# The slots' bias taken into phi before the logits, in place of two bias products per bank

## What is computed

```python
x = x + xattn(layernorm(x), ctx, Wq, Wk, Wv, Wo)         # softmax over 1500 keys, 16 heads
h = layernorm(x)                                          # no affine part: every row sums to 0
logits = (einsum('tzd,ed->tze', h, phi_w) + phi_b).reshape(t, z, 64, 32)
D = softmax(logits, axis=3);  C = softmax(logits, axis=2)
X = einsum('tznp,tzd->npd', D, h)                         # then clip, layernorm, tanh
Y = einsum('npd,ndH->npH', tanh(...), expert_w) + expert_b
x = x + einsum('tznp,npH->tzH', C, Y)
```

## Time and profile before

| | |
|---|---|
| median of 3 runs | 433.64 us |
| the profiled execution: its own time | 433.6 us |
| its span, first to last instruction | 431.7 us |
| PE (TensorE) busy | 422.8 us, 98% |
| DVE (VectorE) busy | 333.9 us, 77% |
| ACT (ScalarE) busy | 245.2 us, 57% |
| POOL (GpSimd) busy | 167.7 us, 39% |
| granted TensorE clock | 1.00 |

### The profile page before, as it was taken

One profiled execution on the slowest core, in us unless ns is written; L12 is line 12 of the kernel. 1 busy time (PEld: TensorE's weight loads), 2 busy tenths in 40 slices (PEclk: granted clock), 3 DMA queues, 4 the chain that ended last, 5 costly groups with the idle time before them and its releaser, 6 DMA issues.

```text
span 431.7 us, 7476 instructions
## 1 busy us (share of the span) xinstructions
PE 422.8 (98%) x3004; PEld 388.5 (90%) x3004; DVE 333.9 (77%) x612; ACT 245.2 (57%) x412; POOL 167.7 (39%) x98
## 2 busy tenths in 40 slices
PE   7999999999999999999999999999999999999897
PEld 5898999999999999889999998899999898999887
DVE  3788756875786778767898689978988899669981
ACT  2576647665664546654673766466655564644641
POOL 6409800524050405032608053617146443456710
DMA  7401110213020011110120012101000010296000
GB/s 203 143 16 14 33 58 14 57 44 100 14 53 33 20 14 22 64 18 14 14 73 20 12 14 72 20 12 15 2 18 14 0 14 18 53 260 176 2 2 23
DMA packets 15418, 19.05 MB, mean 44 GB/s; under 512 B 4032, under 2 KB 10960, under 8 KB 15384
## 3 DMA queue, kind: packets, MB, share of 16 engines
q1 hardware_dynamic: 15384, 18.58, 17.3%
HBM read 18.32 MB, written 0.26 MB: 43 GB/s over the span
## 4 chain that ended last, share of the span: by engine, by line
PE 82%; DVE 11%; ACT 5%; DMA 1%; issue 0%; SPq 0%; ACTq 0%
PE turned L736 16%; PE acc L756 8%; PE acc L757 8%; PE acc L758 8%; PE scores L720 8%; PE scores L726 8%; PE scores L723 8%; PE misc L773 3%; PE misc L642 2%; DVE pT_l L1424 2%; ACT prob L1170 2%; DVE small L1414 2%; PE scores L1100 2%; PE misc L800 2%; ACT logit L1221 1%; ACT pT_h L1163 1%
## 5 line engine op out<-in xcount | busy, mean ns | idle before, releaser
L1163 ACT CAST pT_h<-turned 125x512 fp32r<-125x512 f32 x168 | 95.3, 591 | 124.1 <-PE turned L736 123.5
L1424 DVE TENSOR_TENSOR pT_l<-turned,pT_h 125x512 fp32r<-125x512 f32 x168 | 112.3, 686 | 60.2 <-ACT pT_h L1163 59.5
L1414 DVE TENSOR_REDUCE small<-scores 128x1 f32<-128x500 f32 x168 | 108.1, 674 | 4.4 <-PE scores L726 4.1
L736 PE MATMUL turned<-ident,prob 128*125 128x128 f32 x672 | 94.6, 276 | 1.9 <-DVE pT_l L1424 1.6
L736 PEld LDWEIGHTS turned<-ident,prob 128*125 128x125 f32 x672 | 87.5, 187 | 9.5 <-DVE pT_l L1424 3.5
L756 PE MATMUL acc<-pT_h,ctx_nh 125*128 125x256 f32 (+1 forms) x288 | 94.1, 327 | 0.0
L1170 ACT ACTIVATE prob<-scores,small 128x1500 f32<-128x1500 f32 x56 | 85.0, 1518 | 10.2 <-DVE small L1417 9.8
L758 PE MATMUL acc<-pT_h,ctx_nl 125*128 125x256 f32 (+1 forms) x288 | 86.5, 300 | 0.0
L757 PE MATMUL acc<-pT_l,ctx_nh 125*128 125x256 f32 (+1 forms) x288 | 86.3, 300 | 0.0
L720 PE MATMUL scores<-ctx_th,qk_h 128*128 128x500 f32 x168 | 67.7, 403 | 0.4 <-ACT prob L1170 0.4
L726 PE MATMUL scores<-ctx_th,qk_l 128*128 128x500 f32 x168 | 65.3, 389 | 0.0
(11 more groups left out here) (216 smaller groups left out, 567.8 us busy)
## 6 DMA issues: line engine op xcount, KB each, us to landing
ctx_raw<-in_ctx_dram SPq DMA_DIRECT2D x7, 750.0 KB
rbc<-rden_row SPq DMA_DIRECT2D x15, 128.0 KB, 3.3
rbc<-rden_row SPq DMA_DIRECT2D x8, 192.0 KB, 3.2
eb<-in_L_ffn_expert_b_dram SPq DMA_DIRECT2D x4, 256.0 KB, 5.6
ctx_raw<-in_ctx_dram SPq DMA_DIRECT2D x3, 224.0 KB, 4.9
wq_sb<-in_L_xattn_Wq_dram SPq DMA_DIRECT2D x2, 256.0 KB, 4.6
wk_sb<-in_L_xattn_Wk_dram SPq DMA_DIRECT2D x2, 256.0 KB, 5.2
wv_sb<-in_L_xattn_Wv_dram SPq DMA_DIRECT2D x1, 512.0 KB, 3.7
```

What stands on the lines that cost most here:

```text
L736: last = tr(turned[0:CK, m, 128 * c:128 * c + 128], prob[u][:, CK * j:CK * j + CK], ident[:, :])
L1163: nc.scalar.copy(pT_h[0:CK, PLACES[g // NT % 2][t], CPB * k:CPB * k + CPB, :], turned[0:CK, (KB * u + k) % 2, :].rearrange("p (c r) -> p c ...
L1414: m = v.tensor_reduce(bankmax[:, u, k:k + 1], scores[:, k, 0:KW], AX.X, ALU.max)
L1424: v.tensor_tensor(pT_l[0:CK, place, dst, :], turned[0:CK, (KB * u + k) % 2, :].rearrange("p (c r) -> p c r", c=CPB), pT_h[0:CK, place, dst ...
```

## The change

`pick`, `b_raw`, `b_hl`, their five semaphore steps and the two L808 products of each of the 16 logits banks go. Instead, the constant 1 is added to every normalised row as it is copied out of PSUM, and each slot's row of phi_w gets an offset, off = (phi_b - sum of the row) / 128, before it is transposed. Since a normalised row h sums to 0, (h + 1) . (phi + off) = h . phi + sum(phi) + 128 off = h . phi + phi_b.

For the offset there are now: one DMA of phi_b as 16 rows of 128, a TensorE transpose of it in step (2,0), two VectorE sums over phi_sb in steps (2,0) and (2,1) and a subtraction, and on GpSimd, behind `split_qk(3)`, one small multiplication and four additions over 512 columns each. `turn_phi` waits for these. ScalarE's copy of the turned rows becomes an `add` of 1.0, and the low part `lo_x2nT` adds 1.0 too.

The diff, without the names of tiles and semaphores that only go or come:

```diff
@@ -92,8 +90,8 @@
         zero = sb("zero", [128, 1])
         neghalf = sb("neghalf", [128, NQ])
         x_sb = sb("x_sb", [PT, NQ, D])
-        b_hl = sb("b_hl", [128, BW], F32R)
-        pick = sb("pick", [128, BR], F32R)
+        b_rows = sb("b_rows", [NS, 128])
+        phi_off = sb("phi_off", [128, NS])
         x2n = sb("x2n", [PT, NQ, D])
         lnbuf = sb("lnbuf", [PT, NQ, 6])
         lnmv = sb("lnmv", [PT, NQ, 2])
@@ -398,9 +396,7 @@
                 sp.dma_start(rbc[:, 0:128 * w], row.partition_broadcast(128)).then_inc(rbc_in, 16)
             load_ctx(1)
-            sp.wait_ge(bias_zero, 1)
-            for p in (0, 32):
-                sp.dma_start(b_raw[p:p + BR, :], phi_b.rearrange("(c e) -> c e", c=BR)).then_inc(bias_in, 16)
+            sp.dma_start(b_rows[:, :], phi_b.rearrange("(k p) -> k p", p=128)).then_inc(bias_in, 16)
             for b in range(B):
                 if b > 0:
                     spread_rden(NG * b, (b + 1) % 2, 2)
@@ -435,8 +431,6 @@
             gp.affine_select(out=ident[:, :], in_=ident[:, :], compare_op=ALU.not_equal,
                              fill=1.0, base=0, pattern=[[-1, 128]],
                              channel_multiplier=1).then_inc(ident_ready, 1)
-            pool.wait_ge(ident_ready, 1)
-            gp.tensor_tensor(pick[:, :], ident[:, 0:BR], ident[:, 32:32 + BR], ALU.add).then_inc(pick_ready, 1)
             def split_ctx(b, a, first=False):
@@ -492,6 +486,18 @@
                 gp.tensor_tensor(xa_l[:, PT:NA], xnT[:, PT:3 * PT], xa_h[:, PT:NA].bitcast(F32),
                                  ALU.subtract).then_inc(xa_lo, 1)
+            def centre_phi():
+
+
+                pool.wait_ge(phi_dif, 1)
+                gp.tensor_scalar(phi_off[:, :], phi_off[:, :], 1.0 / D, None, ALU.mult).then_inc(phi_mean, 1)
+                pool.wait_ge(phi_mean, 1)
+                for n in range(LC):
+                    ks = slice(4 * n, 4 * n + 4)
+                    gp.tensor_tensor(phi_sb[:, ks, :], phi_sb[:, ks, :],
+                                     phi_off[:, ks].unsqueeze(2).broadcast_to([128, 4, D]),
+                                     ALU.add).then_inc(phi_mid, 1)
+
             def split_phi():
                 pool.wait_ge(x2n_dve, SPLIT_Q + 1)
@@ -565,7 +571,6 @@
                 gp.tensor_tensor(xt_nb[:, ks], xt_nb[:, ks], xt_rs[:, ks], ALU.mult).then_inc(nb_pool, 1)
-            gp.memset(b_raw[:, :], 0.0).then_inc(bias_zero, 1)
             root(0, 0, 1)
             root(1, 1, NQ)
             pool.wait_ge(ln_rs, 2)
@@ -578,16 +583,10 @@
             split_weights()
             split_ctx(1, 1)
             split_xa()
-            pool.wait_ge(bias_in, 32)
-            gp.tensor_tensor(b_hl[:, :], b_raw[:, :], zero[:, :].broadcast_to([128, BW]),
-                             ALU.add).then_inc(bias_hi, 1)
-            pool.wait_ge(bias_hi, 1)
-            gp.tensor_tensor(b_hl[32:64, :], b_raw[32:64, :], b_hl[32:64, :].bitcast(F32),
-                             ALU.subtract).then_inc(bias_lo, 1)
-            pool.wait_ge(bias_lo, 1)
             split_ctx(2, 0)
             split_qk(2)
             split_qk(3)
+            centre_phi()
             split_ctx(3, 1)
             root(2, 0, 1)
             split_qk(4)
@@ -777,6 +776,7 @@
             def turn_phi(n, k):
+                pe.wait_ge(phi_mid, n + 1)
                 for c in range(4):
                     last = tr(bank(k)[:, 128 * c:128 * c + 128], phi_sb[:, 4 * n + c, :], ident[:, :])
                 last.then_inc(phi_pe, 1)
@@ -797,16 +797,12 @@
                 o = bank(LOGIT_BANKS[q][c])[0:PT, :]
                 cols = slice(512 * c, 512 * c + 512)
                 if q < SPLIT_Q:
-                    mm(o, x2nT[:, PT * q:PT * q + PT], phiT[:, cols], start=True, stop=False)
+                    last = mm(o, x2nT[:, PT * q:PT * q + PT], phiT[:, cols], start=True, stop=True)
                 else:
                     pe.wait_ge(phi_lo, c + 1)
                     mm(o, x2h[:, q - SPLIT_Q, :], phi_h[c][:, :], start=True, stop=False)
                     mm(o, x2l[:, q - SPLIT_Q, :], phi_h[c][:, :], start=False, stop=False)
-                    mm(o, x2h[:, q - SPLIT_Q, :], phi_l[:, cols], start=False, stop=False)
-                for e in range(512 // BW):
-                    row = 512 // BW * c + e
-                    last = mm(o[:, BW * e:BW * e + BW], pick[:, row:row + 1].broadcast_to([128, PT]),
-                              b_hl[:, :], start=False, stop=(e == 512 // BW - 1))
+                    last = mm(o, x2h[:, q - SPLIT_Q, :], phi_l[:, cols], start=False, stop=True)
                 last.then_inc(logit_pe, 1)
             def mid_step(b, t):
@@ -865,8 +861,11 @@
                     ahead_head(14, 1)
                     pe.wait_ge(ahead_act, 14)
                     ahead_head(15, 0)
+                if b == 2 and t == 0:
+                    pe.wait_ge(bias_in, 16)
+                    pe.wait_ge(ahead_act, HEADS)
+                    tr(misc[:, 1, 0:NS], b_rows[:, :], ident[0:NS, 0:NS]).then_inc(bias_pe, 1)
                 if b == 2 and t == 2:
-                    pe.wait_ge(phi_in, 16)
                     turn_phi(0, M1)
                 if b == 2 and t == 3:
                     pe.wait_ge(phi_cp, 1)
@@ -881,8 +880,6 @@
                     pe.wait_ge(ctxT_lo, KB * (b + 2))
                     pe.wait_ge(x2nT_act, i)
                     pe.wait_ge(phi_cp, LC)
-                    pe.wait_ge(bias_lo, 1)
-                    pe.wait_ge(pick_ready, 1)
                     logits(i - 1, 0)
                 if b in (3, 5) and t == 5:
                     pe.wait_ge(logit_act, LC * (i - 1) + 1)
@@ -1190,7 +1187,7 @@
             def copy_x2nT(q, k):
                 act.wait_ge(x2nT_pe, q + 1)
                 dst = x2nT[:, PT * q:PT * q + PT] if q < SPLIT_Q else x2h[:, q - SPLIT_Q, :]
-                nc.scalar.copy(dst, bank(k)[:, 0:PT]).then_inc(x2nT_act, 1)
+                nc.scalar.add(dst, bank(k)[:, 0:PT], 1.0).then_inc(x2nT_act, 1)
             def copy_logits(q, c):
                 act.wait_ge(logit_pe, LC * q + c + 1)
@@ -1460,8 +1457,8 @@
             def lo_x2nT(q, k):
                 dve.wait_ge(x2nT_act, q + 1)
-                v.tensor_tensor(x2l[:, q - SPLIT_Q, :], bank(k)[:, 0:PT], x2h[:, q - SPLIT_Q, :].bitcast(F32),
-                                ALU.subtract).then_inc(x2l_dve, 1)
+                v.scalar_tensor_tensor(x2l[:, q - SPLIT_Q, :], bank(k)[:, 0:PT], 1.0,
+                                       x2h[:, q - SPLIT_Q, :].bitcast(F32), ALU.add, ALU.subtract).then_inc(x2l_dve, 1)
             def by_expert(ap):
                 return ap.rearrange("p (n s) -> p n s", s=P_SLOT)
@@ -1536,8 +1533,19 @@
                 dve.wait_ge(last_dsum, c + 1)
                 v.reciprocal(sm, sm).then_inc(last_drec, 1)
+            def sum_phi(part):
+                dve.wait_ge(phi_in, 16)
+                ks = slice(NS // 2 * part, NS // 2 * part + NS // 2)
+                v.tensor_reduce(phi_off[:, ks], phi_sb[:, ks, :], AX.X, ALU.add).then_inc(phi_sum, 1)
+                if part:
+                    dve.wait_ge(bias_pe, 1)
+                    dve.wait_ge(phi_sum, 2)
+                    v.tensor_tensor(phi_off[:, :], misc[:, 1, 0:NS], phi_off[:, :], ALU.subtract).then_inc(phi_dif, 1)
+
             def ffn_step(b, t):
+                if b == 2 and t <= 1:
+                    sum_phi(t)
                 if b in (2, 4, 6) and t == 6:
                     residual((b - 2) // 2)
                 if b in (3, 5, 7) and t == 0:
```

More of the change, by code:

```diff
@@ L62, in xattn_softmoe_kernel @@
     LC = SLOTS // 512
-    BW = 256
-    BR = SLOTS // BW
     assert ROWS == NT * 128 and NT == 7 and M == NC * CK and KW <= 512 and D == 128
@@ L192, in xattn_softmoe_kernel @@
         phi_sb = at("phi_sb", [128, NS, D], F32, phi_at)
-        b_raw = at("b_raw", [128, BW], F32, logit1_at + 2 * QKB)
         logit = [logit0, logit1, at("logit2", [PT, SLOTS], F32, t0_at), at("logit3", [PT, SLOTS], F32, t1_at + KB8)]
@@ L278, in xattn_softmoe_kernel @@
         eb_in = sem("eb_in")
[L279 to L282, removed]
+        bias_pe = sem("bias_pe")
+        phi_sum = sem("phi_sum")
+        phi_dif = sem("phi_dif")
+        phi_mean = sem("phi_mean")
+        phi_mid = sem("phi_mid")
         phi_pe = sem("phi_pe")
```

## The result

| | before | changed |
|---|---|---|
| median of 20 runs each, side by side | 433.46 us | 431.35 us |
| lowest to highest of these | 431.86 to 434.36 | 429.81 to 432.73 |
| profiled execution, own time (span) | 433.6 (431.7) | 429.94 (428.2) |

The ratio is 0.9952, with a 95% interval of 0.9939 to 0.9965: 2.1 us less (1.5 to 2.6), a little more than the 0.3% that can be told from no change. 431.6 was forecast, within 430.3 to 433.0.

The account below looks back on a forecast made before the run. TensorE, busy 98%, was taken as the bound, with VectorE close behind and holding some hand-overs. Gains of 2.30 us, less 0.10 for the transpose and 0.24 for the `add`, net 1.96: 433.6 to 431.6 us, range 430.3 to 433.0.

Parts of the forecast that it names:

- every pair counts: Rival, all 16 logits banks: VectorE's chain shortens with TensorE's, all 3.76 us gained; 430.2 us, chance 0.15.
- Group 0: Logits banks of steps (3,4) to (4,0): all four bias-product pairs count in full, 0.94 us gained.
- Group 1: Logits banks of steps (5,4) to (6,0): bank 0 gains nothing, banks 1 to 3 count, 0.70 us.
- Group 2: Logits banks of steps (7,2), (7,3): only what VectorE can save counts, 0.42 us of 0.94.
- Its slack is 0.18 before 346.97, 0.12 in the maxima, and 0.18 before 353.61: VectorE around (7,2), (7,3): slack of 0.48 us, less 0.06 for a hand-over, leaves 0.42.
- a wait of about 1.3 us near 360: Expected sign in the changed profile: TensorE's wait near 360 grows from 0.78 to about 1.3 us.
- Group 3: Logits banks behind the loop: one pair counts, three are hidden under VectorE; 0.24 us gained.
- The transpose: TensorE's added 16-column bias transpose, in a stretch without gaps: costs 0.10 us, range 0 to 0.2.
- The `add`: Replaces ScalarE's copy of turned rows: 0.12 us more, on the path in (7,1) and behind the loop.
- The bias pair: Two bias products in each of 16 logits banks: 0.235 us of TensorE time a pair.
- Sums on VectorE, GpSimd's additions, phi_sb: Work added in (2,0), (2,1) and on GpSimd fits idle time, phi_sb lands in time: cost 0.
- VectorE holds nearly everything: Rival: groups 1 and 2 give nothing, additions cost their upper ends; 433.1 us, chance 0.17.

Follow-up runs that it names:

- the bare bank: The kernel before with the two bias products left out only in group 1's bank 0, step (5,4); 434.92 us in its one timed run.
- sum earlier: The changed kernel with VectorE's second sum of group 0's exponentials (1.21 us) moved from step (5,4) to (5,1); median 430.35 us, ratio 0.9934 to the kernel before.

## Why the prediction was right, and where its terms were not

- **TensorE is the bound, but not every pair counts.** Right: 2.58 us of 3.76 reach the end; 2.30 was forecast.
- **Group 0, 0.94.** Measured 0.91 to 0.93. Long shares and low parts that are early: all four pairs lie on TensorE alone.
- **Group 1, 0.70 with bank 0 at nothing.** Measured 0.72 and 0.00. The reason is shown twice: by the bare bank (0.03 us), and by the sum moved away (0.20 us back). It was to be seen only in the timeline, as a load 0.06 us behind a low part in a stretch in which VectorE has no idle time. TensorE's list of waits didn't have it. The load alone isn't the sign: group 0's first bank ends at such a load too, with VectorE waiting in between, and it counted in full.
- **Group 2, 0.42: mis-sized.** It was 0.69 to 0.71. The step that failed is "Its slack is 0.18 before 346.97, 0.12 in the maxima, and 0.18 before 353.61", from which a hand-over's 0.06 was taken as well. The starts moved by 0.26 and 0.38 = 0.64, since each wait that goes gives back an overlap of 0.08 beside its idle time. The sign "a wait of about 1.3 us near 360" was wrong for another reason: a hand-over in (7,4) was overlooked. TensorE there, before and after:

```profile
354.18 0.28 PE L758 MATMUL acc<-pT_h,ctx_nl 125*128 125x256 f32 x1
354.36 0.70 PE L736 MATMUL turned<-ident,prob 128*125 128x128 f32 x4
```

```profile
350.66 0.28 PE L757 MATMUL acc<-pT_h,ctx_nl 125*128 125x256 f32 x1
351.10 0.70 PE L735 MATMUL turned<-ident,prob 128*125 128x128 f32 x4 [0.16 <-DVE pT_l L1421]
...
357.09 0.70 PE L735 MATMUL turned<-ident,prob 128*125 128x128 f32 x4 [0.71 <-DVE pT_l L1421]
```

  The transpose follows the product after 0.44 us in place of 0.18: TensorE spends 0.26 us of its 0.94 here, waiting for the low part that ends at 351.05, and 0.69 reach the end. The next hand-over comes 5.99 us later in both kernels, with a wait of 0.71 us, against 0.78 before. That VectorE, and not TensorE, sets the group was right: 0.69 and not 0.94.
- **Group 3, 0.24.** One of four pairs; measured 0.23 to 0.26. VectorE's maxima of these banks, which answer to the earlier trace rows:

```profile
385.64 0.69 DVE L1524 TENSOR_REDUCE dmax<-turned 112x16 f32<-112x512 f32 x1 [1.04 <-PE turned L805]
...
386.97 0.68 DVE L1524 TENSOR_REDUCE dmax<-turned 112x16 f32<-112x512 f32 x1
```

  The wait for the first bank fell from 1.27 to 1.04, and the second maximum follows 1.33 us later (1.37 before): the other three pairs stay under VectorE.
- **The transpose, 0.10: mis-sized.** It cost 0.36, above its upper end of 0.2. The failed step is "this one is smaller": the price was read from a stretch of like transposes, and a small one among large ones costs more than a large one, which cost 0.10, near the row's 0.13.
- **The `add`, 0.12 twice: mis-sized.** It was 0.01, under which both stages came out as if it cost nothing. The row of the tanh was the wrong neighbour, and the price lay at the range's lower end. By the Trainium skill (ScalarE: Activation LUTs, What ACT_TABLE_LOAD costs) it would be an estimated 279 ns without a pointer operand; this trace has 253 to 263, nearer to it than to the 372 with one. Which form the `add` has, no run shows.
- **The bias pair, 0.235.** Right in groups 0 and 1 (0.91 / 4 and 0.72 / 3: 0.23, 0.24). The 98 ns estimated from the Trainium skill (TensorE: Matmul & The Clock Gate, Back-to-back issue gap) would have made it 0.20; the trace doesn't agree, here as in the earlier trace rows.
- **Sums on VectorE, GpSimd's additions, phi_sb: 0.** Right, with the signs as listed. GpSimd's additions took 1.01 us each and not 0.92; the idle time covered that.

The misses are +0.27 for group 2, -0.26 for the transpose, +0.22 for the `add` and 0.01 for the other groups together: 1.96 came out as 2.2, and by the medians as 2.1. That the sum fitted to 0.3 us owes something to their signs. The range took in the measured values for group 2 and the `add`, but not the transpose's 0.36.

Three slips in the prediction's working change nothing above. The bounds 430.8 and 432.7 come out only with the transpose's ends, 0 and 0.2, which aren't named among them (without these they are 430.9 and 432.6). The rival "VectorE holds nearly everything" leaves out VectorE's own upper end of 0.3 us, with which it gives 433.4. And TensorE's list of waits has one more in the main loop, 0.39 us for ScalarE at 34.60, which the change doesn't touch.

## What to carry to other kernels

Where two engines run close to full, ask of every instruction that goes which hand-over comes next and who is late there. A weight load 0.05 us behind its releaser shows who releases it, which a list of waits need not; whether a saving is lost there is decided by the releaser's idle time since the hand-over before, and none means that it is. Between two such hand-overs the gain is what the releasing engine's starts can move, idle time and lost overlaps together. And compare profiles step by step: where the start alone varies by more than the effect, the difference of two spans says nothing.

## What the runs showed that was not expected

- A 16 x 16 transpose in a stream of full-sized products costs 0.36 us (0.16 itself, and 0.42 instead of 0.23 for the product behind it); three of them together 0.50; a 128 x 128 transpose in the same place 0.10.
- The time to the first exponential varies from 15.04 to 17.86 us over 14 executions, and by 2.2 us (15.68 and 17.86) between two kernels that are the same up to there. The end varies too: from the start of the last VectorE instruction to the end of the span it is 2.29 to 2.40 us in 13 of the executions and 3.84 in one (sum earlier, 432.94 us). The runs of one kernel spread by as much (431.86 to 434.36 before); that these two make up most of it is likely, but only one execution of each kernel, and two of the changed one, can be looked into.
- Moving one 1.21 us sum by three steps is worth 0.20 us in one of two kernels that differ by pairs of products, and -0.03 in the other.
